# One turn of a test-time learning loop: another order of the work on every engine, the large weight update in halves, two gradients in pairs of batches

## The reference, cut to what matters

```python
def _mlp(params, h):
    for w1, w2 in params:
        h = h + jax.nn.gelu(h @ w1) @ w2
    return h
...
def assoc_loss(p, k, v):
    pred = _mlp(p, k)
    return jnp.mean((pred - v) ** 2)
...
def step(carry, x_t):
    params, mom = carry
    k = _l2norm(x_t @ Wk)
    v = x_t @ Wv
    ...
    g = grad_fn(params, k, v)

    def upd_m(m, gg):
        sh = (B,) + (1,) * (m.ndim - 1)
        return eta.reshape(sh) * m - lr.reshape(sh) * gg
    ...
    def upd_p(p, nm):
        sh = (B,) + (1,) * (p.ndim - 1)
        return p * (1.0 - forget.reshape(sh)) + nm
```

## Time and profile before

| | us |
|---|---|
| median of three runs | 999.18 (995.9 to 999.75) |
| the profiled execution | 1000.6 |
| its span, all engines | 998.8 |
| 31 products that close A0: first, last | 96.93, 562.52 |

### The profile page before, as it was taken

How to read it: one execution, slowest core, us unless ns; L and a number is a source line. 1 busy time by engine, 2 the same in 40 slices (tenths; PEclk the granted TensorE clock), 3 DMA queues, 4 the chain that set the end, 5 groups by cost and what they waited for, 6 DMA issues and landing times. The chain is left out here.

```text
span 998.8 us, 24052 instructions
## 1 busy us (share of the span) xinstructions
PE 756.4 (76%) x7837; PEld 476.0 (48%) x7837; DVE 722.1 (72%) x1821; ACT 617.7 (62%) x1382; POOL 587.0 (59%) x760
## 2 busy tenths in 40 slices
PE   2967888888888888888888859956475522999960
PEld 2554445444454444444444424421164421899950
DVE  4485887888878788787887862669777771777747
ACT  3656777777777777777777723228543321988840
POOL 0145777677776777867768749820006674466660
PEclk8887999999999999999999959977855555999995
DMA  7009999990000000000000024014001112233317
GB/s 229 1 2 206 158 204 140 9 4 0 0 0 0 0 0 0 0 0 0 0 0 0 0 53 118 1 54 135 3 1 41 48 51 59 69 94 89 95 52 250
DMA packets 105404, 54.07 MB, mean 54 GB/s; under 512 B 42624, under 2 KB 96664, under 8 KB 105360
## 3 DMA queue, kind: packets, MB, share of 16 engines
q1 hardware_dynamic: 98976, 43.34, 27.8%
q0 software_dynamic: 4544, 9.38, 2.9%
q10 hardware_dynamic: 1840, 0.79, 0.3%
HBM read 21.49 MB, written 29.44 MB: 51 GB/s over the span
## 5 line engine op out<-in xcount | busy, mean ns | idle before, releaser
L528 DVE SCALAR_TENSOR_TENSOR l_m<-l_m,l_eta,lp_g 128x256 f32<-128x256 f32 x512 | 219.5, 476 | 46.5 <-PE lp_g L641 26.0
L383 POOL TENSOR_TENSOR s_w<-l_kw,l_m 128x512 f32<-128x512 f32 x192 | 238.3, 1277 | 12.3 <-DVE l_m L528 12.3
L476 ACT ACTIVATE l_kw<-s_w,l_keep_lr 128x256 f32<-128x256 f32 x384 | 171.3, 507 | 0.0
L1333 POOL DMA_INDIRECT f_yg<-f_yr,f_xmeta x78 | 78.4, 1005 | 54.5 <-DVE f_yr L1663 41.7
L1328 POOL DMA_INDIRECT f_xg<-f_xrow,f_place x64 | 63.3, 989 | 54.3 <-DVE f_place L1559 35.7
L469 ACT COPY l_wt<-lp_b 128x512 f32<-128x512 f32 x96 | 56.4, 588 | 27.8 <-PE lp_b L634 27.8
L1308 ACT ACTIVATE f_hh<-fp_v,f_bcol 128x256 f32<-128x256 f32 x156 | 61.2, 476 | 13.1 <-PE fp_v L1428 9.7
L388 POOL TENSOR_TENSOR l_kw<-s_w,l_keep 128x512 f32<-128x512 f32 x64 | 65.1, 1035 | 0.0
L634 PE MATMUL lp_b<-s_cst,s_w 128*128 128x128 f32 x384 | 62.2, 285 | 2.2 <-ACT s_w L515 1.3
L634 PEld LDWEIGHTS lp_b<-s_cst,s_w 128*128 128x128 f32 x384 | 43.3, 142 | 32.1 <-ACT l_wt L469 13.7
L1428 PE MATMUL fp_v<-f_xf,s_w_hi 128*128 128x256 bf16 x312 | 55.4, 280 | 1.4 <-DVE f_xmeta L1643 1.0
(11 more groups left out here) (320 smaller groups left out, 1998.0 us busy)
## 6 DMA issues: line engine op xcount, KB each, us to landing
f_xg<-s_pad SPq DMA_DIRECT2D x1, 17280.0 KB, 107.1
f_xt<-f_xg SPq DMA_DIRECT2D x39, 130.0 KB
r_w<-in_L_ffn_W_dram SPq DMA_DIRECT2D x16, 256.0 KB, 3.1
s_w<-f_yg SPq DMA_DIRECT2D x16, 256.0 KB, 3.8
xs<-in_x_dram SPq DMA_DIRECT2D x4, 512.0 KB, 6.9
t_w<-in_L_ffn_W_dram SPq DMA_DIRECT2D x8, 256.0 KB
out_dram<-s_x SPq DMA_DIRECT2D x8, 256.0 KB, 3.1
s_xsh<-s_xl SPq DMA_DIRECT2D x4, 448.0 KB, 3.5
```

Of the source, the lines that this page charges most:

```text
L383: nc.gpsimd.tensor_tensor(W[k][:, half(h), :], KW[k][:, half(h), :], M[k][:, half(h), :], ALU.add).then_inc(w_ready[k], 1)
L476: m = nc.scalar.mul(KW[k][:, b, :], W[k][:, b, :], keep_lr[:, b:b + 1])
L528: i = nc.vector.scalar_tensor_tensor(out=M[k][:, b, :], in0=M[k][:, b, :], scalar=eta[:, b:b + 1], in1=ps_g[b][:, 0:256], op0=ALU.mult, op ...
L1333: nc.gpsimd.indirect_dma_start(sb["yg"][:, :], bass.IndirectOffsetOnAxis(ap=xmeta[:, j, a, 0:1].bitcast(mybir.dt.int32), axis=0), yr[j % R ...
```

## The change

No product, momentum or update is added or left out. The update of W20 and two gradients are cut, and on every engine the order is another:
- `update` for "20" works on two batches at a time; the momenta of M20 (0, 1) move ahead of da0, and the first half of the update follows da0 at once.
- dW11 and dW20 are computed for batches 0, 1 and then 2, 3, with down DH1 between the pairs of the one and up b and ke between those of the other. `grad_done` is counted six times a step instead of four.
- up b with dh1f goes ahead of ke; down H1 goes ahead of the second `turn_w` of "21"; the first `turn_w` of "11" goes ahead of turn g1.
- dd gets a function of its own (`weighted`), and dd1 is computed behind dp. The momenta of M21 and M10 stand apart, with da1, gp0 and u1 between them.
- ScalarE's keeping products are single batches in another order; the copy of wt20's first half goes ahead of dpf.
- GpSimd's adds and keeping products are halves in another order, and keep_lr waits for all keeping products of the step before.

The diff, cut (GpSimd's, ScalarE's, VectorE's and TensorE's parts in this order; left out are new forms of `add`, `keep_of` and `momentum`, which only take one half or fewer batches):

```diff
+                    if steps:
+                        if grads:
+                            for k in ("21", "20", "10"):
+                                pool.wait_ge(kept[k], p * 2 + 2)
+                            pool.wait_ge(kept["11"], p * 2 + 2)
+                        nc.gpsimd.tensor_copy(keep_lr[:, :], step_of(t, "coef")[:, 4:9]).then_inc(lr_in, 1)
+                        pool.wait_ge(lr_in, t + 1)
+                        nc.gpsimd.tensor_tensor(keep[:, :], keep_lr[:, 0:B], none[:, :], ALU.subtract).then_inc(keep_in, 1)
                     if grads:
-                        pool.wait_ge(kept["11"], p * 2 + 2)
-                        add(p, "11", G11)
+                        add(p, "21", G21, 1)
                     if steps:
-                        pool.wait_ge(mm_done, t * 7 + A0)
...
+                            pool.wait_ge(grad_done, p * 6 + D10)
+                        nc.gpsimd.tensor_copy(kc[:, :], step_of(t, "ktok")).then_inc(kc_ready, 1)
+                    if grads:
+                        add(p, "11", G11, 1)
+                    if steps:
+                        keep_of(t, "11", 0)
+                    if grads:
+                        add(p, "10", G10, 0)
+                    if steps:
                         nc.gpsimd.tensor_copy(kx[:, :], step_of(t + 1, "kf")).then_inc(kx_ready, 1)
...
-                        keep_of(t, "11")
                         if grads:
                             pool.wait_ge(mom_ready, mom(p, G10, 1))
                         nc.gpsimd.tensor_copy(eta[:, :], step_of(t, "coef")[:, 0:4]).then_inc(eta_in, 1)
-                        nc.gpsimd.tensor_copy(kc[:, :], step_of(t, "ktok")).then_inc(kc_ready, 1)
+                        pool.wait_ge(mm_done, t * 7 + A0)
+                        pool.wait_ge(kx_ready, t + 1)
                         pool.wait_ge(eta_in, t + 1)
                         scaled(ke, eta).then_inc(ke_ready, 1)
+                        scaled(kk, keep).then_inc(kk_ready, 1)
+                        keep_of(t, "11", 1)
                     if grads:
-                        pool.wait_ge(kept["10"], p + 1)
-                        add(p, "10", G10)
+                        add(p, "10", G10, 1)
...
+                    add(t, "21", G21, 0)
+                    if not last:
+                        pool.wait_ge(mm_done, t * 7 + A0)
+                        nc.gpsimd.tensor_tensor(sk[:, :].rearrange("p (b c) -> p b c", b=B), sb["kdot"][:, bass.ds(t, 1), :].to_broadcast([128, B, C]),
+                                                sb["cst"][:, C_MEAN:C_MEAN + 128].rearrange("p (b c) -> p b c", b=B), ALU.mult).then_inc(sk_ready, 1)
+                    add(t, "11", G11, 0)
...
+                    keep_of(t, "21", 0)
                     hidden(t, 0, ps_a)
...
+                    tanh(t, 0, ps_a)
+                    keep_of(t, "21", 2)
                     wt(t, X21B, "21", 1)
-                    tanh(t, 0, ps_a)
                     feature(t, TH1, h1f, 128)
-                    keep_of(t, "21", (1,))
                     wt(t, X20B, "20", 1)
...
+                    keep_of(t, "21", 1)
+                    wt(t, X20A, "20", 0)
                     feature(t, TDP, dpf, 128, 0.5)
-                    wt(t, X20A, "20", 0)
-                    keep_of(t, "21", (2, 3))
+                    keep_of(t, "10", 0)
+                    keep_of(t, "20", 0)
+                    keep_of(t, "10", 1)
                     wt(t, X11B, "11", 1)
                     feature(t, TDA1, daf, 256)
-                    keep_of(t, "20", range(B))
+                    keep_of(t, "20", 1)
+                    keep_of(t, "21", 3)
+                    keep_of(t, "20", 2)
+                    keep_of(t, "20", 3)
                     feature(t, TDH1, dh1f, 128, 0.5)
-                    keep_of(t, "10", range(B))
-
+                    keep_of(t, "10", 2)
+                    keep_of(t, "10", 3)
...
+                def update(t, k, n, h):
+
+                    dve.wait_ge(kept[k], t * 2 + h + 1)
+                    dve.wait_ge(mom_ready, mom(t, n, h))
+                    nc.vector.tensor_tensor(W[k][:, half(h), :], KW[k][:, half(h), :], M[k][:, half(h), :], ALU.add).then_inc(w_ready[k], 1)
...
+                def weighted(t, l):
+                    dve.wait_ge(sq_ready, t * 2 + l + 1)
                     dve.wait_ge(gelu_ready, t * 2 + l + 1)
                     nc.vector.scalar_tensor_tensor(out=dd[l][:, :], in0=q[l][:, :], scalar=1.0 / 3.0, in1=g[l][:, :],
                                                    op0=ALU.add, op1=ALU.mult).then_inc(dd_ready, 1)
...
-                        momentum(p, "20", G20, range(B))
-                        update(p, "20", G20)
+                        update(p, "20", G20, 0)
+                        momentum(p, "20", D20B, (2, 3))
+                        update(p, "20", G20, 1)
...
                     if grads:
-                        momentum(p, "10", G10, (0, 1))
+                        momentum(p, "10", D10, (0,))
+                    if steps:
+                        slope(t, 0, ps_a)
+                    if grads:
+                        momentum(p, "10", D10, (1, 2))
                     if steps:
                         slope_in(t, 1, ps_b)
                     if grads:
-                        momentum(p, "10", G10, (2, 3))
+                        momentum(p, "10", D10, (3,))
...
-                    slope_out(t, 1, ps_b)
-                    momentum(t, "21", G21, (0, 1))
+                    weighted(t, 1)
+                    bent(t, 1, ps_b)
+                    slope(t, 1, ps_b)
+                    momentum(t, "21", D21, (0,))
                     slope_times(t, 1, ps_a, DG1)
-                    momentum(t, "21", G21, (2, 3))
-                    momentum(t, "11", G11, (0, 1))
+                    momentum(t, "21", D21, (1,))
+                    momentum(t, "21", D21, (2, 3))
+                    momentum(t, "11", D11A, (0, 1))
                     dve.wait_ge(mm_done, t * 7 + DH1)
                     nc.vector.tensor_tensor(dh1[:, :], ps_h[:, 0:128], dp[:, :], ALU.add).then_inc(chain, 1)
-                    momentum(t, "11", G11, (2, 3))
+                    momentum(t, "11", D11B, (2, 3))
+                    momentum(t, "20", D20A, (0, 1))
                     slope_times(t, 0, ps_b, DG0)
...
+                        grad_2(g[0], dh1, (2, 3))
                         pe.wait_ge(chain, p * 6 + K_DA0)
...
-                        pe.wait_ge(w_ready["21"], t * 2 + 2)
+                        pe.wait_ge(w_ready["21"], t * 2 + 1)
...
+                        grad_1(kc, da[0], range(B))
                     if steps:
-                        pe.wait_ge(wt_ready, t * 6 + X21A)
-                        turn_w("21", 1)
                         pe.wait_ge(w_ready["20"], t * 2 + 2)
                         pe.wait_ge(gf_ready, t * 6 + TG0)
                         down(ps_h, gf[0], W["20"])
+                        pe.wait_ge(wt_ready, t * 6 + X21A)
+                        pe.wait_ge(w_ready["21"], t * 2 + 2)
+                        turn_w("21", 1)
                         pe.wait_ge(chain, t * 6 + K_H1)
...
+                        pe.wait_ge(slope_ready[0], t * 2 + 2)
+                        turn_w("11", 0)
 
                 def backward(t, last=False):
                     pe.wait_ge(gelu_ready, t * 2 + 2)
                     turn(g[1], 256)
-                    pe.wait_ge(slope_ready[0], t * 2 + 2)
-                    turn_w("11", 0)
...
-                    pe.wait_ge(mom_ready, mom(t, G21, 1))
-                    grad_1(h1, da[1])
+                    pe.wait_ge(mom_ready, mom(t, G21, 0))
+                    grad_1(h1, da[1], (0, 1))
                     pe.wait_ge(wt_ready, t * 6 + X11B)
                     pe.wait_ge(gf_ready, t * 6 + TDA1)
                     down(ps_h, daf, WT["11"])
+                    pe.wait_ge(mom_ready, mom(t, G21, 1))
+                    grad_1(h1, da[1], (2, 3))
                     if not last:
                         pe.wait_ge(w_ready["10"], t * 2 + 2)
                         pe.wait_ge(kk_ready, t + 1)
                         up(ps_a, kk, W["10"], stop=False)
                     pe.wait_ge(chain, t * 6 + K_DH1)
                     turn(dh1, 128)
+                    pe.wait_ge(mom_ready, mom(t, G11, 0))
+                    grad_2(g[0], dh1, (0, 1))
+                    pe.wait_ge(gf_ready, t * 6 + TDH1)
+                    up(ps_b, dh1f, WT["20"])
                     if not last:
                         pe.wait_ge(ke_ready, t + 1)
                         up(ps_a, ke, M["10"], start=False, stop=False)
-                    pe.wait_ge(gf_ready, t * 6 + TDH1)
-                    up(ps_b, dh1f, WT["20"])
```

More of the change, by code:

```diff
@@ L331, in learn @@
         G21, G11, G20, G10 = range(4)
+        D21, D11A, D11B, D20A, D20B, D10 = range(1, 7)
         X21A, X21B, X20B, X11A, X20A, X11B = range(1, 7)
@@ L377, in per_batch, with add, keep_of @@
```

(35 more changed lines are left out.)

30 lines of the change are left out of this document (8 added, 22 removed).

## The result

The changed kernel takes 991.32 us, median of five runs (988.05 to 992.25), against 999.18 before: a ratio of 0.9926, 95% interval 0.9905 to 0.9948, so 7.9 us or 0.7% faster. I had forecast 1002. The time lies in the range, but on the other side of no change.

What follows compares the result with a forecast made beforehand. Bound: a chain through TensorE, each product waiting for something the one before set off, 15.52 us a step. Terms sum to +0.07 a step, +2 over 30, plus 1 at most: 1003.6 profiled, median 1.4 lower, 1002; range 983 to 1030.

Steps and rivals of the forecast that it cites:

- A0 to H1: Step piece from product A0 to down H1: 3.17 us before, forecast 2.3 with the update hidden, -0.87.
- up b to Y: Step piece from up b to down Y: 2.14 us before, +0.14 for the turn of W11 ahead of turn g1.
- Sum +0.07 a step: Total of the nine pieces of a loop step: 0.07 us longer, +2 us over 30 steps.
- rival 3: Pairs of dW11 and dW20 on TensorE cost half: -0.77 us a step, 978 us; chance 0.18.
- DH1 to turn dh1: Step piece on TensorE: 1.26 us before, forecast 1.79 with the pair (2, 3) and kk between, +0.53.
- turn dh1 to up b: Step piece on TensorE: 0.72 us before, forecast 0.92 with the first pair of dW20 between, +0.20.
- up b to A0: Step piece on TensorE: 1.21 us before, forecast 1.67 with ke and the second pair of dW20, +0.46.
- The tie at the update: W20's update: VectorE's first half reckoned ready at 2.18 us, GpSimd's add at 2.19, counted from turn dh1.
- The tie at dd1: VectorE's dd1 reckoned ready at 7.82 us behind A0, GpSimd's keeping product of W11 near 7.85.
- Rival 1: At W20's update GpSimd's add goes first and VectorE's half waits: +0.65 us a step, 1022 us; chance 0.20.
- rival 2: VectorE's dd1 goes second to GpSimd's keeping product, da1 0.7 us late: +21 us, 1023 us; chance 0.12.
- my own case: The main forecast for the whole kernel: 1002 us, own range 996 to 1009 (0.2 a step either way); chance 0.42.

Runs made afterwards that it cites:

- the run with both parts: The changed kernel with GpSimd's add of the second half of W21 ahead of keep_lr and dd1 back behind u1; 986.43 us.

## Why the prediction was wrong

- **What failed is the size of two terms.** "A0 to H1" took "2.3 with the upper end", that is 0.76 for the distance from dW10 to H1, although have 0.65 between dW11 and DH1, the same pair of tile shapes; it is 0.64, and H1 comes at 2.18. "up b to Y" said of the turn of W11 that it "holds TensorE for 0.66, until 1.28", which is the length of a group and not its distance to the next of the same tiles: the turn at 314.84 is followed by turn g1 at 315.40, 0.56 later, at 1.13 behind up b, when g1 was ready. Both took for a distance more than TensorE needs from start to start, and together they make -0.28 of the 0.35 by which the step was over-reckoned. The rest is 0.01 to 0.04 in each of four other pieces, less 0.03 in H1 to up b.
- "Sum +0.07 a step" and with it the sign hung on that: gains of 1.37 against costs of 1.44, reckoned to 0.1 each. With the two terms right it would have been -0.21, some 6 us.
- **Right:** VectorE off the path between A0 and H1 (if by 0.09 only); pairs as long as wholes (0.70 and 0.71), with rival 3 refuted; DH1 to turn dh1, turn dh1 to up b and up b to A0 within 0.03. What lies outside the 30 spacings was small, -2.1 of the span instead of +1; in the run with both parts it is another 4.3 lower at equal steps, so it says little.
- **The tie at the update** was there, within 0.05 of the reckoning, and went VectorE's way, which the rows of before could not tell: that is luck. The tie at dd1 was none: VectorE led by 0.24. dd1 came 7.54 behind A0 where 7.82 was reckoned, for the most part by the same two terms, and the keeping product 7.78 where 7.85 was.
- **The rivals' prices** are not measured as they stand. Rival 1's +0.65 is also what the run with keep behind the add shows, but there the add begins 0.22 ahead of the half. Had it won by a hair, VectorE would have waited 0.22 more: 0.87 a step, an estimate. Rival 1 had the second half nearly right and the base, H1 at 2.30, too late. For rival 2 (+0.7) dd1 was only held back by a wait, until 0.13 after a product that begins 0.24 behind it; that costs 1.22 to 1.26 a step, and the clock 1.78 more. Its 0.25 of slack ahead of da1 wasn't there: dd1 ended 1.27 later and dW11 came 1.28 later. A dd1 that loses by a hair would end some 0.74 later (1.04 - 0.15 + 0.42 against 0.57, an estimate); whether the clock falls then no run shows.
- **The chances.** That the time lies in the range is luck in part: the low end was there for rival 3, which had 0.18 of the 0.21 for a faster kernel and is refuted. 0.40 on the slower side for two ties was a fair reading of the rows, but the 0.42 of my own case deserved a range that reaches to -0.3 a step, since nine terms with up to 0.16 of error each add up; "0.2 a step either way" was too narrow.

## What to carry to other kernels

On an engine without gaps, add up distances from start to start of neighbours with the same pair of tile shapes, never lengths: 0.12 and 0.16 at two places decided the sign. Where a product waits for an update, add the way between the engines, here 0.13 from the end of the one to the start of the other. Where VectorE reads two inputs in SBUF, find GpSimd's instruction that becomes ready in the same quarter of a microsecond, and order one of them out of the way instead of leaving it to a lead of 0.06. And a part that is late somewhere doesn't help alone: a copy 0.2 earlier gave 0.04 as long as two momenta stood ahead of da1.
